# Storing projected K, V and Q row by row and moving them to the per-head layout with separate HBM-to-HBM transfers

## The reference

```python
q = (hidden_states @ Wq.T).reshape(b, t, H, D)     # H = 16, D = 128
k = (hidden_states @ Wk.T).reshape(b, t, H, D)
v = (hidden_states @ Wv.T).reshape(b, t, H, D)
q = _feature_map(q, gamma, beta)                   # layer norm over D of x * gamma + beta
k = _feature_map(k, gamma, beta)
q = q * D ** (-0.5)
attn = jnp.einsum('bqhd,bkhd->bhqk', q, k) ** 2    # then causal mask
o = jnp.einsum('bhqk,bkhd->bqhd', attn, v)
o = o / (sum of attn + EPS);  return o @ Wo.T
```

## Time and profile before

| | us |
|---|---|
| runs, median (5371.61 to 5390.24, 2 runs) | 5380.93 |
| profiled execution, own time | 5359.81 |
| its span, core 7, the slowest | 5358.3 |
| spans of cores 0 to 3 | 5278.6 to 5295.1 |
| spans of cores 4 to 7 | 5342.8 to 5358.3 |

### The profile page before, as it was taken

The page is one execution under the profiler, slowest core; times in us unless marked ns, Lnnn a source line. Parts: engine busy times, 40 slices in busy tenths (PEclk is TensorE's granted clock), DMA queues, the critical chain, the costliest instruction groups (busy, mean ns, idle before and its releaser), DMA issues.

```text
span 5358.3 us, 52829 instructions; the slowest of 8 cores (5278.6 to 5358.3 us)
## 1 busy us (share of the span) xinstructions
PE 3161.4 (59%) x13416; PEld 1290.9 (24%) x13416; DVE 1846.5 (34%) x3416; ACT 1815.6 (34%) x2685; POOL 514.5 (10%) x964
## 2 busy tenths in 40 slices
PE   1555555555555555333234666777789989812799
PEld 0222222222222222111111111222234334301334
DVE  0333333333333333244442331212226666433221
ACT  0222222222222222122223444555424444364451
POOL 1111122111111111100000000000000000000000
PEclk9777777777777777665557888999889999855788
DMA  9222222222222222633322112111347666445785
GB/s 173 79 79 79 79 81 81 87 83 83 79 79 79 79 79 71 141 91 98 93 76 68 54 45 91 59 67 67 97 139 235 230 235 234 148 151 159 264 287 193
DMA packets 269201, 628.24 MB, mean 117 GB/s; under 512 B 134256, under 2 KB 142448, under 8 KB 236912
## 3 DMA queue, kind: packets, MB, share of 16 engines
q0 software_dynamic: 80896, 327.22, 20.7%
q1 hardware_dynamic: 188016, 297.65, 17.0%
HBM read 573.34 MB, written 84.93 MB: 123 GB/s over the span
## 4 chain that ended last, share of the span: by engine, by line
PE 40%; DVE 14%; ACT 13%; DMA 12%; issue 11%; POOL 3%; SPq 3%; another core or an unknown queue 2%; DVEq 1%; ACTq 1%; POOLq 0%
PE kv_ps L355 21%; PE dps L1118 4%; PE ops L689 3%; POOL vsc L80 3%; PE gps L893 3%; ACT s2t L672 3%; SPq L80 3%; PE ups L905 2%; DMA wfp<-gwt_r 2%; DMA hgr<-hgscr 2%; PE zps L693 2%; DVE s2t L674 2%; PE sps L661 2%; PE wops L814 2%
## 5 line engine op out<-in xcount | busy, mean ns | idle before, releaser
L355 PE MATMUL kv_ps<-wk_sb,xnT 128*128 128x512 bf16 x2560 | 654.7, 424 | 169.1 <-DMA wv_sb<-wvt 89.7
L355 PE MATMUL kv_ps<-wv_sb,xnT 128*128 128x512 bf16 x2048 | 530.5, 428 | 354.8 <-DVE kg L365 354.8
L330 PE MATMUL tp_ps<-ident,xnb 128*128 128x128 bf16 x640 | 69.4, 271 | 850.7 <-ACT xnT L336 703.4
L274 ACT ACTIVATE sgn<-wfp 128x1024 bf16<-128x1024 f32 x264 | 278.9, 1056 | 663.5 <-DMA wfp<-gwt_r 476.8
L689 PE MATMUL ops<-s2t,vsb 128*128 128x512 bf16 x768 | 309.5, 403 | 274.0 <-DVE s2t L674 224.2
L674 DVE TENSOR_TENSOR s2t<-s2t,msk_sb 128x512 bf16<-128x512 bf16 x512 | 217.6, 425 | 648.1 <-ACT s2t L672 643.8
L672 ACT ACTIVATE s2t<-sps 128x512 bf16<-128x512 f32 x512 | 305.8, 597 | 338.7 <-PE sps L661 331.8
L355 PEld LDWEIGHTS kv_ps<-wk_sb,xnT 128*128 128x128 bf16 x2560 | 270.1, 107 | 543.8 <-issue 332.1
L893 PE MATMUL gps<-terng,xqs 128*128 128x512 bf16 x1408 | 347.4, 404 | 61.9 <-DVE ternu L761 44.4
L1118 PE MATMUL dps<-dtern,hqts 128*128 128x512 bf16 x1408 | 356.3, 422 | 34.2 <-DMA hqts<-hqtd 31.4
L355 PEld LDWEIGHTS kv_ps<-wv_sb,xnT 128*128 128x128 bf16 x2048 | 217.6, 107 | 657.4 <-issue 495.9
(11 more groups left out here) (139 smaller groups left out, 3690.4 us busy)
## 6 DMA issues: line engine op xcount, KB each, us to landing
wfp<-gwt_r POOLq DMA_DIRECT2D x176, 512.0 KB, 4.7
wfpt<-gwt_r POOLq DMA_DIRECT2D x88, 1024.0 KB, 6.6
wfp<-dwt_r POOLq DMA_DIRECT2D x88, 512.0 KB, 4.2
xqs<-xqsc SPq DMA_DIRECT2D x88, 512.0 KB, 4.9
wfpt<-dwt_r POOLq DMA_DIRECT2D x44, 1024.0 KB, 7.3
hqts<-hqtd SPq DMA_DIRECT2D x32, 1408.0 KB, 8.1
xf<-xfull SPq DMA_DIRECT2D x32, 1024.0 KB, 8.1
hgscr<-hgb SPq DMA_DIRECT2D x88, 256.0 KB, 2.7
```

What stands on the lines that cost most here:

```text
L274: lambda e, sl=slot, t=tgt, cc=col: e.activation(wabs_dump[:], wfp[sl][:], ACT.Abs, accum_out=t[:, cc:cc + 1]), waits=[s_abs[slot]])
L330: TE(lambda e, bb=bank, f=fc, jj=j, s=src_bf: e.transpose(bb[:, jj * 128:(jj + 1) * 128], s[:, f * 128:(f + 1) * 128], ident[:]), waits=wl ...
L355: TE(lambda e, jj=j, f=fc, w=w_sb: e.matmul(kv_ps[jj][:], xnT[:, f * 128:(f + 1) * 128], w[:, f * DM + jj * 512: f * DM + (jj + 1) * 512], ...
```

## The change

K, V and q are no longer written straight to the per-head layout. There are three new HBM tensors, `kscr`, `vscr`, `qscr`, of one contiguous 128 x 2048 block per tile. Each group of four heads goes out in one store of 128 x 512 (rows of 1 KB), and V in one store of 128 x 2048, which is now issued by SP. The stores of `xqsc` are merged in the same way, with the layout of that tensor unchanged. A new helper `relayout_kv(t0)` copies K and V of four tiles from the new tensors to `ksc` and `vsc`, in 32 DMAs issued by POOL; it is emitted after the head transposes in tiles 4, 8, ..., 28, ahead of that tile's first `emit_abs(2)`, and once more after the loop. `relayout_q` does the same for q in 16 DMAs, in the fifth own tile and after the own-tile loop. The first DMA of a relayout waits for all stores issued so far. POOL waits for the end of all relayouts ahead of the barrier after the own-tile loop. Attention reads as before.

```diff
+            if wide_fn is not None:
+                b.dma("sync", wide_fn(g), ktb[kslot][:, 0:512],
                       s_ktb[kslot], waits=[(CTR[ck[0]], ck[1])])
...
+    def relayout_q(s0):
+        wl = [s_ktb[0], s_ktb[1]]
+        for h in range(H):
+            b.dma("gpsimd", qsc[h, :, s0:s0 + 4, :],
+                  qscr[s0:s0 + 4, :, h * 128:(h + 1) * 128]
+                  .rearrange("t p c -> p t c"), s_rl,
+                  waits=(wl if h == 0 else []))
+
+    def relayout_kv(t0):
+        wl = [s_ktb[0], s_ktb[1], s_kvw[0], s_kvw[1]]
+        for h in range(H):
+            b.dma("gpsimd", ksc[h, :, t0:t0 + 4, :],
+                  kscr[t0:t0 + 4, :, h * 128:(h + 1) * 128]
+                  .rearrange("t p c -> p t c"), s_rl,
+                  waits=(wl if h == 0 else []))
+            b.dma("gpsimd", vsc[h, :, t0:t0 + 4, :],
+                  vscr[t0:t0 + 4, :, h * 128:(h + 1) * 128]
+                  .rearrange("t p c -> p t c"), s_rl)
...
-            head_transposes_store(kfm_ring[(t - 1) % 2], pfm,
-                                  lambda h, tt=t - 1: ksc[h, :, tt, :])
+            head_transposes_store(kfm_ring[(t - 1) % 2], pfm, None,
+                                  wide_fn=lambda g, tt=t - 1:
+                                  kscr[tt][:, g * 512:(g + 1) * 512])
             kfm_free2[(t - 1) % 2] = [(cT, cT.n)]
+            if t % 4 == 0:
+                relayout_kv(t - 4)
         emit_abs(2)
...
-        for h in range(H):
-            b.dma("gpsimd", vsc[h, :, t, :], xnb[slot][:, h * 128:(h + 1) * 128],
-                  s_kvw[slot], waits=[(cS, sck)])
+        b.dma("sync", vscr[t], xnb[slot][:], s_kvw[slot], waits=[(cS, sck)])
...
+    relayout_kv(NT - 4)
...
+            if s == 4:
+                relayout_q(0)
...
+    relayout_q(4)
+
+    b.wait("sync", s_ktb[0], s_ktb[1], s_kvw[0], s_kvw[1])
+    b.wait("gpsimd", s_rl)
     b.barrier(bar)
```

More of the change, by code:

```diff
@@ L122, in build_nc @@
     ksc = nc.dram_tensor("ksc", [H, 128, NT, 128], BF16, kind="Internal").ap()
+    kscr = nc.dram_tensor("kscr", [NT, 128, DM], BF16, kind="Internal").ap()
+    vscr = nc.dram_tensor("vscr", [NT, 128, DM], BF16, kind="Internal").ap()
+    qscr = nc.dram_tensor("qscr", [NOWN, 128, DM], BF16, kind="Internal").ap()
     vsc = nc.dram_tensor("vsc", [H, 128, NT, 128], BF16, kind="Internal").ap()
@@ L395, in featuremap, with head_transposes_store @@
         return last
-    def head_transposes_store(src_bf, src_ck, dst_fn):
+    def head_transposes_store(src_bf, src_ck, dst_fn, wide_fn=None):
         for g in range(4):
@@ L422, in head_transposes_store @@
             st["tp_evac"][g % 2] = ck
-            for j in range(4):
-                h = g * 4 + j
-                b.dma("sync", dst_fn(h), ktb[kslot][:, j * 128:(j + 1) * 128],
+            if wide_fn is not None:
+                b.dma("sync", wide_fn(g), ktb[kslot][:, 0:512],
                       s_ktb[kslot], waits=[(CTR[ck[0]], ck[1])])
+            else:
+                for j in range(4):
+                    h = g * 4 + j
+                    b.dma("sync", dst_fn(h), ktb[kslot][:, j * 128:(j + 1) * 128],
+                          s_ktb[kslot], waits=[(CTR[ck[0]], ck[1])])
             st["ktb_free"][kslot] = s_ktb[kslot].n
@@ L467, in build_nc @@
         sck = cS.n
-        for h in range(H):
-            b.dma("gpsimd", vsc[h, :, t, :], xnb[slot][:, h * 128:(h + 1) * 128],
-                  s_kvw[slot], waits=[(cS, sck)])
+        b.dma("sync", vscr[t], xnb[slot][:], s_kvw[slot], waits=[(cS, sck)])
         st["xnb_free"][slot] = [(s_kvw[slot], s_kvw[slot].n)]
         emit_abs(2)
-    head_transposes_store(kfm_ring[(NT - 1) % 2], pend1[0],
-                          lambda h: ksc[h, :, NT - 1, :])
+    head_transposes_store(kfm_ring[(NT - 1) % 2], pend1[0], None,
+                          wide_fn=lambda g: kscr[NT - 1][:, g * 512:(g + 1) * 512])
     kfm_free2[(NT - 1) % 2] = [(cT, cT.n)]
+    relayout_kv(NT - 4)
     ck_ph1_mm = cT.n
@@ L514, in build_nc @@
             pslot, pqb, pfm = pend[0]
[L515 to L516 removed]
+            head_transposes_store(kfm_ring[pslot], pfm, None,
+                                  wide_fn=lambda g, ss=s - 1:
+                                  qscr[ss][:, g * 512:(g + 1) * 512])
             kfm_free2[pslot] = [(cT, cT.n)]
[L518 to L519 removed]
+            head_transposes_store(xnb[pslot], pqb, None,
+                                  wide_fn=lambda g, ss=s - 1:
+                                  xqsc[ss].rearrange("p f c -> p (f c)")
+                                  [:, g * 512:(g + 1) * 512])
             st["xnb_free"][pslot] = [(cT, cT.n)]
+            if s == 4:
+                relayout_q(0)
         if s + 1 < NOWN:
@@ L556, in build_nc @@
     pslot, pqb, pfm = pend[0]
[L557 to L560, removed]
+    head_transposes_store(kfm_ring[pslot], pfm, None,
+                          wide_fn=lambda g: qscr[NOWN - 1]
+                          [:, g * 512:(g + 1) * 512])
+    head_transposes_store(xnb[pslot], pqb, None,
+                          wide_fn=lambda g: xqsc[NOWN - 1]
+                          .rearrange("p f c -> p (f c)")
+                          [:, g * 512:(g + 1) * 512])
     st["xnb_free"][pslot] = [(cT, cT.n)]
-    b.wait("sync", s_ktb[0], s_ktb[1])
-    b.wait("gpsimd", s_kvw[0], s_kvw[1])
+    relayout_q(4)
+    b.wait("sync", s_ktb[0], s_ktb[1], s_kvw[0], s_kvw[1])
+    b.wait("gpsimd", s_rl)
     b.barrier(bar)
@@ L635, in build_nc @@
     msk_free = 0
+    b.wait("sync", s_rl)
     for C in range(2):
```

1 line of the change is left out of this document (added).

## The result

| | us |
|---|---|
| before, median of 10 runs (5308.97 to 5390.24) | 5348.23 |
| after, median of 11 runs (5150.84 to 5253.44) | 5206.85 |
| after / before | 0.9715, 95% interval 0.9658 to 0.9772 |
| profiled execution of after, own time | 5238.34 |
| its spans, all cores | 5158.8 to 5236.8 |

The changed kernel is faster by 2.9% (0.0285 x 5348.23 = 152 us); the forecast was 128 us, 2.4%, which lies inside the interval. Core 3 was the slowest in the profiled execution; I read core 7, whose rows of before are shown above, and core 0.

What follows compares the result with a forecast made beforehand. A chain through several engines, with ACT waiting for `wfp` loads held behind POOL's V stores, bounds the tile loop. Gains 461 and losses 333 give net -128 us, 5380.9 becoming 5253; range 5110 to 5580.

Steps and rivals of the forecast that it cites:

- V's wait goes: Tile ends of the tile loop: V's store on SP removes ACT's wait for `wfp` loads, 12.1 us a tile, 384 us.
- the fourth rival: Tile ends: half the gain on V's wait is lost, `wfp` load colliding with `xf` load; net +64, 5445 us, chance 0.06.
- K's faster slot turn: K's head transposes: 4 stores instead of 16 bring ACT's second copy earlier, 1.4 us x 31 = 43 us.
- The stall: Every fourth tile: relayout issues on POOL delay ACT's `wfp` loads, 40.4 us each, 7 times in the loop, 283 us.
- X: POOL's time per relayout DMA, taken as 1.07 us, the geometric mean of bounds 0.54 and 2.15.
- the prediction's own formula: Whole kernel: net change in us is 288X - 437, with X as POOL's time per relayout DMA.
- The piece on the DMA engines: Relayout of four tiles: 17 ns per 256-byte piece, 1024 pieces per engine, 17 us, under POOL's 34.
- The third rival: DMA engines drain the relayout slowly, `wfp` load behind it; at 89 ns a piece +381, 5760 us; chance 0.12.
- The ends: Eighth relayout before the barrier: wq loads 31 us later; own-tile loop gains 34 us, q relayouts lose 4 and 15.
- The first rival: Relayout issue: pieces cost POOL nothing, X = 0.54; net -276, 5105 us; chance 0.22.
- The second: Relayout issue: POOL pays per piece, X = 2.15, slower; net +183, 5564 us; chance 0.20.
- One sign that I had set: Stages after 2830 us: a change by more than noise would make the whole account wrong.

Runs made afterwards that it cites:

- the first experiment: The kernel before with one word changed, V's 16 small stores issued by SP instead of POOL, no relayout or wide stores: 4965.07 us, ratio 0.9177.
- The three kernels named in the section on the result: The changed kernel with the relayout in four quarters (4902.65 us), wholly behind the tile loop (5102.64 us), or of eight tiles each (5117.67 us).
- the direct stores: The kernel before with V's stores on SP, four staging slots instead of two, wide `xqsc` stores and no relayout: 4811.99 us, ratio 0.9024.

## Why the prediction was right

The forecast was a difference of two larger terms. Both were tested apart.

- **V's wait goes** (predicted 12.1 us a tile, 384 in all): shown by the first experiment, 13.1 a tile. The prediction read 386.4 us in 32 waits as one per tile, and left out the `dwt_r` row; with it the sum is 425.8. The gap of the earlier trace rows has the right size. In the changed kernel some of the wait comes back at the tile ends: 50 us in the whole loop of core 0, 1.6 a tile, where V's stores alone left 21. That the V store and the `xf` load delay the second `wfp` load fits the order of starts, and would be the fourth rival in small, but no run took them apart.
- **K's faster slot turn** (predicted 1.4 us a tile): the turn itself shortened by 1.8. With the two together an ordinary tile of core 0 went from 64.9 to 51.3 us (mean of 23), 13.6 where 13.5 was said; V's stores alone gave 13.2. So the quicker turn shows as 0.4 us of the tile. The longer `wfp` waits take about 1 us of it, and where the rest goes is not shown.
- **The stall** (predicted 32 x 1.07 + 6.2 = 40.4 us): the seven long tiles of core 0 have a mean of 88.9, so 88.9 - 51.3 = 37.6 each, 263 in all against 283. The place and the kind of the stall were right; its size came out right by luck, from terms that were wrong one by one. *X was mis-sized*: 0.741, not the geometric mean 1.07, which makes 23.7 us and not 34.2. *The hold was not in the sum at all*: POOL stood for another 3.7 us before the 32nd DMA (3.4 to 7.2 on the cores read). And the last K store took 3.85 instead of 2.2 us to free POOL, and the load behind the pieces 6.0 instead of 4.1; why these two took longer is not shown. With the true X the prediction's own formula gives 288 x 0.741 - 437 = -224 us, some 70 us more gain than was measured, and V's wait at its true size would have made the miss larger.
- **The piece on the DMA engines** (taken as 17 ns): 22 ns of engine time in the relayout behind the loop, and 31 DMAs of after landed 25.8 us after the first was issued (580.27 to 606.1), 26 ns a piece with the landing time. The 17 of the earlier trace rows was for stores from SBUF. So the engines' floor was not 17 us beneath POOL's 34 but about as high as POOL's 23.7, and in this kernel it still adds nothing but the hold. The third rival, an engine side so slow that the load lands behind it, did not come true here, where the engines stood empty when the load was issued. With 1024 pieces per DMA the drain did set the stall, by way of the holds.
- **The ends**: 27.8 us of relayout before the barrier (2029.04 to 2056.86 on core 7), where 32X was 34.2. The own-tile loop of core 0 gained 15.1, where 34 - 4 - 15 = 15 was said; in the kernels with the relayout in quarters and behind the loop, whose own-tile loop is the same, it gained 19 and 21. On core 7 its end came 18.9 us after DVE's last copy:

```profile
2652.51 0.42 DVE L422 COPY sgn<-tp_ps 128x512 bf16<-128x512 bf16 x1 [2.33 <-DMA xqsc<-sgn]
2655.32 11.77 POOL L80 DMA_DIRECT2D qsc<-qscr  x16 [19.41 <-DMA xqsc<-sgn]
2671.43 0.34 DVE L609 TENSOR_REDUCE wabs_r<-wabs_g 128x16 f32<-128x176 f32 x1 [18.49 <-POOLq L96]
```

The first rival (X = 0.54) had the nearer X but not its consequence: without the hold and with the other short terms it gave -276. The second, POOL pays per piece, is refuted: 0.2 to 0.3 ns, not 4.2 (0.537 us / 128). The Trainium skill (DMA: Bandwidth & Descriptors, section "Anatomy of one DMA — SWDGE (gpsimd) path") says that many descriptors can be emitted before the added cost shows. In POOL's instruction time this held, 0.741 us for 512 pieces against 0.537 for 128. With 1024 pieces the holds were the dearer part, 31.5 of 59.4 us for 32 DMAs.

One sign that I had set seems to fail: the stages after 2830 us were to stay within noise, and in the profiled execution core 0's grew by 28 us at a lower granted clock, core 7's by 11. The three kernels named in the section on the result have the same later stages and show -12 to +4 us on core 0, so the sign holds.

## What to carry to other kernels

A wait for a load can be an order problem: look at what stands between the pass that frees the slot and the load in the issuing engine's queue. Here one word, 16 issues on another in-order queue, was worth 8%, and the same 32 issues cost 37 us ahead of a needed load and next to nothing in quarters behind it. Where the issues can hide, as here on SP, store straight into the layout that the reader wants. A second trip through HBM in 256-byte pieces is paid for in issues and in the holds between them, and more staging slots bought a quicker slot turn without it.

## What the runs showed of the hardware

- A DMA with a three-dimensional pattern of 256-byte pieces costs POOL 0.688, 0.741 and 0.878 us for 256, 512 and 1024 pieces. Eight times the pieces of a V store (128, two-dimensional, 0.537) cost 1.6 times as much. SP took a median of 0.75 us for the 512, and up to 5.3.
- HBM to HBM in 256-byte pieces, on all eight cores at once, took 22 ns of engine time a piece, against 17 for stores of the same size from SBUF. Where POOL issued faster than the engines could follow, 960 pieces per engine took 29.3 us from the first issue to the last landing.
- POOL was held before the DMA that would bring the queue to about a thousand pieces per engine (after 992 and after 960), never with 256 pieces a DMA. Each hold ended 0.5 to 0.7 us after everything issued had landed: 3.4 to 7.2 us with 512 pieces a DMA, where the engines kept pace, and 10 to 17 us with 1024.
- A shorter tile loop came with a higher granted clock. Over the tile loop of core 0 it was 0.76 before, 0.78 after, 0.83 with V's stores alone moved and 0.84 with the direct stores, for the same matmuls. PE's busy time there was 1066, 1051, 1053 and 1074 us, so the clock explains at most some 15 us of the gains.
